# Ranking edges inside a graph network: one copy of the running counts per group, and keys compared with all earlier chunks

## The reference

```python
def spmm(z):
    return jax.ops.segment_sum(edge_weight[:, None] * z[col], row, num_segments=N)
z = x
y = z @ weights[0]
for k in range(1, Kh):          # Kh = 4: three hops
    z = spmm(z)
    y = y + z @ weights[k]
```

## Time and profile before

| what | value |
|---|---|
| median of three runs | 9740.51 us |
| profiled execution, its own time: the span from first to last instruction (nothing around it is recorded) | 12913.0 us |
| stage src_scatter (ranking and scatter by source) | 160 to 1475 us of the span |
| first hop (no ranking) | 1490 to 2720 us |
| second hop, hop1 (100 rankings) | 2734 to 4040 us |
| third hop, hop2 (96 rankings) | 4050 to 5385 us |
| busy share of the span: POOL, PE, DVE, ACT | 54%, 53%, 51%, 16% |

### The profile page before, as it was taken

How to read it: one execution, slowest core, us unless ns; L and a number is a source line. 1 busy time by engine, 2 the same in 40 slices (tenths; PEclk the granted TensorE clock), 3 DMA queues, 4 the chain that set the end, 5 groups by cost and what they waited for, 6 DMA issues and landing times. The chain is left out here.

```text
span 12913.0 us, 169378 instructions
## 1 busy us (share of the span) xinstructions
PE 6851.3 (53%) x37679; PEld 5969.4 (46%) x37680; DVE 6544.7 (51%) x22687; ACT 2092.6 (16%) x6216; POOL 7007.4 (54%) x7417
## 2 busy tenths in 40 slices
PE   6555444445554555356125555566664666655554
PEld 4454333335553555232014445466663556654444
DVE  6444455555555555434125555655555444455555
ACT  4222100001110111011001111222222111122222
POOL 6555566646664666554755555245553455535554
PEclk6555555566666666578557777777777555566676
DMA  0000011111111111223122222111113111122222
GB/s 19 1 1 1 19 45 44 45 42 42 42 42 39 42 42 42 46 70 99 43 48 74 74 74 74 48 35 39 39 39 82 34 37 39 38 53 77 78 79 74
DMA packets 436020, 614.60 MB, mean 48 GB/s; under 512 B 176561, under 2 KB 312069, under 8 KB 435109
## 3 DMA queue, kind: packets, MB, share of 16 engines
q0 software_dynamic: 257024, 486.93, 15.0%
q1 hardware_dynamic: 178305, 119.49, 3.3%
q10 hardware_dynamic: 292, 3.41, 0.1%
HBM read 520.17 MB, written 89.19 MB: 47 GB/s over the span
## 5 line engine op out<-in xcount | busy, mean ns | idle before, releaser
L1098 POOL DMA_INDIRECT hop_rows<-hops,k_src_gather x1568 | 1483.1, 946 | 1037.1 <-issue 438.7
L1149 PE MATMUL hop_sums<-hop_rows,hop_weighted 128*128 x4992 | 1136.9, 399 | 1004.9 <-DVE k_x L1196 678.1
L1149 PEld LDWEIGHTS hop_sums<-hop_rows,hop_weighted 128*128 128x128 f32 x4992 | 990.5, 295 | 1093.3 <-issue 1092.3
L1470 POOL DMA_INDIRECT l_pass_rows<-left_table,k_dst_other x832 | 788.2, 947 | 889.6 <-DVE l_pass_terms L1842 488.2
L1965 POOL DMA_INDIRECT l_weigh_rows<-row_table,l_weigh_ring x832 | 813.3, 978 | 737.8 <-ACT l_weigh_ring L1929 481.4
L1470 POOL DMA_INDIRECT l_pass_rows<-related,k_dst_typed x832 | 787.8, 947 | 740.8 <-DVE l_pass_terms L1842 457.3
L1470 POOL DMA_INDIRECT l_pass_rows<-key_table,k_src_gather x784 | 741.3, 946 | 770.9 <-DVE l_pass_scores L1779 404.8
L728 POOL DMA_INDIRECT src_sorted<-src_scatter_records,src_scatter_places x784 | 752.6, 960 | 583.3 <-DVE src_scatter_places L716 362.5
L1565 PE MATMUL l_pass_sums<-l_pass_zero 128*128 128x272 bf16 (+1 forms) x1210 | 261.2, 305 | 1489.8 <-DVE l_total L1659 1020.4
L1320 POOL DMA_INDIRECT dst_sorted<-rec,dst_places x768 | 760.3, 990 | 525.7 <-issue 225.4
L1098 POOL DMA_INDIRECT hop_rows<-in_x,k_src_gather x784 | 741.4, 946 | 455.0 <-issue 221.0
(11 more groups left out here) (468 smaller groups left out, 18337.5 us busy)
## 6 DMA issues: line engine op xcount, KB each, us to landing
related<-l_tables_rows SPq DMA_DIRECT2D x50, 1024.0 KB
hop_rows<-hops,k_src_gather POOLq DMA_INDIRECT x1568
l_pass_rows<-related,k_dst_typed POOLq DMA_INDIRECT x832
l_pass_rows<-left_table,k_dst_other POOLq DMA_INDIRECT x832
l_weigh_rows<-row_table,l_weigh_ring POOLq DMA_INDIRECT x832
src_sorted<-src_scatter_records,src_scatter_places POOLq DMA_INDIRECT x784
hop_rows<-in_x,k_src_gather POOLq DMA_INDIRECT x784
dst_sorted<-rec,dst_places POOLq DMA_INDIRECT x784
```

The source lines that it names most:

```text
L1098: nc.gpsimd.indirect_dma_start(rows[:, s * G + g, :], None, table_in, bass.IndirectOffsetOnAxis(ap=o.gather[:, c:c + 1], axis=0),).then_in ...
L1149: last = nc.tensor.matmul(sums[:, b, g, :], weighted[:, s % SLOTS, g, :], rows[:, bass.ds(slots[g], 1), :], start=True, stop=True)
L1470: nc.gpsimd.indirect_dma_start(rows[:, s, g, :], None, table, bass.IndirectOffsetOnAxis(ap=index[:, c:c + 1], axis=0),).then_inc(got[s], 16)
```

## The change

In the three rankings (src_scatter, hop1, hop2) the counts are copied once for a group instead of once for a chunk. TensorE adds all four chunks to the counts in a row and raises one signal, and looks all four up in the copy that was made ahead of the group, with one signal. The lookups therefore no longer hold the chunks of the same group, and the comparison makes up for that: chunk g's keys are compared with the key rows of chunks 0 to g, with a mask that is all ones for chunks ahead and the triangle for its own (`k.earlier_ones`). The result tile `same` becomes 16-bit. In a hop, the key rows and the transposes for the next ranking move from TensorE's first half (even step, ahead of chunk 1) to its second half (odd step), behind that step's products.

```diff
@@ scatter_edges and hop: the comparison (VectorE)
-                        nc.vector.scalar_tensor_tensor(out=same[:, g, :], in0=keyrow[:, b, g, :],
-                                                       scalar=records[:, s, g, 0:1], in1=k.before[:],
+                        nc.vector.scalar_tensor_tensor(out=same[:, g * (g + 1) // 2 * P:(g + 1) * (g + 2) // 2 * P],
+                                                       in0=keyrow[:, b, 0:g + 1, :].rearrange("p g j -> p (g j)"),
+                                                       scalar=records[:, s, g, 0:1],
+                                                       in1=k.earlier_ones[:, (G - 1 - g) * P:G * P],
@@ hop: ScalarE, one ranking
-                    for g in range(G):
-                        if g == G - 1:
-                            turn_onehots(r + 1, 1 - b)
-
-                        act.wait_ge(next_ready, r * G + g + 1)
-                        act.wait_ge(looked, r * G + g + 2 * G - 1)
-                        nc.scalar.copy(next_sb[:, g % 2, :], next_ps[:, 0:HIS]).then_inc(next_copied, 1)
+                    act.wait_ge(next_ready, r + 2)
+                    act.wait_ge(looked, r + 2)
+                    nc.scalar.copy(next_sb[:, 1 - b, :], next_ps[:, 0:HIS]).then_inc(next_copied, 1)
+                    turn_onehots(r + 1, 1 - b)
@@ hop: TensorE, rank_columns
                 if half == 0:
+                    pe.wait_ge(next_copied, r + 1)
+                    for g in range(G):
+                        last = nc.tensor.matmul(next_ps[:, 0:HIS], oh_lo[:, s, g, :], oh_hi[:, s, g, :], start=False,
+                                                stop=False, skip_group_check=True)
+                    last.then_inc(next_ready, 1)
+
                     pe.wait_ge(lo_t, r + 1)
                     pe.wait_ge(ranked, r + 1)
-                for g in range(2 * half, 2 * half + 2):
...
+                    for g in range(G):
+                        last = nc.tensor.matmul(nexts[:, b, g, 0:HIS], oh_lo_t[:, b, g, :], next_sb[:, b, :], start=True,
+                                                stop=True)
+                    last.then_inc(looked, 1)
+                else:
+
+                    pe.wait_ge(taken, r + 1)
+                    pe.wait_ge(onehots, r + 2)
+                    pe.wait_ge(matched, r + 2)
+                    for g in range(G):
+                        last = nc.tensor.transpose(keyrow[:, g, :], column[:, b, g:g + 1].to_broadcast([P, P]), k.ident[:])
+                    last.then_inc(rows_ok, 1)
```

More of the change, by code:

```diff
@@ L172, in _ @@
                                     base=0, pattern=[[-1, P]], channel_multiplier=1)
-            nc.gpsimd.affine_select(out=k.before[:], in_=k.before[:], compare_op=ALU.is_gt, fill=0.0,
+            nc.gpsimd.affine_select(out=k.before, in_=k.before, compare_op=ALU.is_gt, fill=0.0,
                                     base=0, pattern=[[-1, P]], channel_multiplier=1).then_inc(made, 1)
@@ L515, in _ @@
     def _(pe):
-        nc.tensor.transpose(turned[:], k.before[:], k.ident[:]).then_inc(pe_step, 1)
+        nc.tensor.transpose(turned[:], k.before, k.ident[:]).then_inc(pe_step, 1)
         pe.wait_ge(d, 2)
@@ L589, in scatter_edges @@
         picked = sb("picked", [P, G, HIS])
-        same = sb("same", [P, G, P])
+        same = sb("same", [P, sum(range(G + 1)) * P], BF16)
         base = sb("base", [P, 2, G])
@@ L659, in _ @@
                     for g in range(G):
[L661 to L674, removed]
+                        last = nc.tensor.matmul(nexts[:, b, g, 0:HIS], oh_lo_t[:, b, g, :], next_sb[:, b, :], start=True,
+                                                stop=True)
+                    last.then_inc(looked, 1)
+                    pe.wait_ge(taken, n + 1)
+                    pe.wait_ge(onehots, n + 2)
+                    for g in range(G):
+                        last = nc.tensor.transpose(keyrow[:, b, g, :], records[:, s, g, 0:1].to_broadcast([P, P]), k.ident[:])
+                    last.then_inc(rows, 1)
+                    turn_onehots((s + 1) % SLOTS)
         @block.vector
@@ new lines, in rank_columns @@
+                    for g in range(G):
+                        last = nc.tensor.matmul(nexts[:, b, g, 0:HIS], oh_lo_t[:, b, g, :], next_sb[:, b, :], start=True,
+                                                stop=True)
+                    last.then_inc(looked, 1)
+                else:
+                    pe.wait_ge(taken, r + 1)
+                    pe.wait_ge(onehots, r + 2)
+                    pe.wait_ge(matched, r + 2)
+                    for g in range(G):
+                        last = nc.tensor.transpose(keyrow[:, g, :], column[:, b, g:g + 1].to_broadcast([P, P]), k.ident[:])
+                    last.then_inc(rows_ok, 1)
+                    for g in range(G):
+                        last = nc.tensor.transpose(turned[:, 1 - b, g, :], oh_lo[:, (s + 1) % SLOTS, g, :], k.identb[:])
+                    last.then_inc(turned_ok, 1)
@@ L1211, in rank_same @@
                 for g in range(G):
-                    last = nc.vector.scalar_tensor_tensor(out=same[:, g, :], in0=keyrow[:, g, :],
-                                                          scalar=column[:, b, g:g + 1], in1=k.before[:],
+                    last = nc.vector.scalar_tensor_tensor(out=same[:, g * (g + 1) // 2 * P:(g + 1) * (g + 2) // 2 * P],
+                                                          in0=keyrow[:, 0:g + 1, :].rearrange("p g j -> p (g j)"),
+                                                          scalar=column[:, b, g:g + 1],
+                                                          in1=k.earlier_ones[:, (G - 1 - g) * P:G * P],
                                                           op0=ALU.is_equal, op1=ALU.mult,
```

59 lines of the change are left out of this document (25 added, 34 removed).

## The result

| | median | lowest to highest | runs |
|---|---|---|---|
| before | 9742.35 us | 9735.38 to 9761.99 | 4 |
| after | 9971.19 us | 9960.04 to 9973.62 | 4 |

The change makes the kernel 2.3% slower: the ratio, estimated from all the runs, is 1.0228, with a 95% interval of 1.0216 to 1.0241; the two medians lie 229 us apart. The profiled execution of after has a span of 9958.3 us, so its idle times are, other than those of the recording before (12913.0 us), those of the runs.

What follows compares the result with a forecast made beforehand. POOL's indirect DMAs were taken to bound the kernel, 9.42 us a pair of steps. A 10.5 us loop gave 196 x (10.5 - 9.42) = 212 us on 9740.5, about 9950 us; range 9735 to 10110, the forecast's own 9800 to 10090.

Steps and rivals of the forecast that it cites:

- POOL bounds before, and the recording's waits are not in the runs: All three ranking stages: POOL issues indirect DMAs nearly without a break, 9.42 us for a pair of steps in a hop.
- Longer comparisons, 0.67 us taken: VectorE in each ranking: 768 more columns at 0.87 ns each, so comparisons go from 1.09 to 1.76 us.
- One copy and one signal worth nothing: ScalarE makes one copy instead of four, TensorE three hand-overs less; at POOL's pace worth nothing in the runs.
- src_scatter unchanged: src_scatter: VectorE's 3.7 us and TensorE's 3.8 us plus at most 0.6 a group stay below POOL's 5.04; nothing changes.
- faster: Rival, chance 0.11: real chunk-by-chunk waits go, 90 us vanish in src_scatter if a quarter is real; 9650 us.
- The two engines take turns: Hops: VectorE 3.90 us, then TensorE 6.84 us, a loop of 10.74 us over POOL's 9.42; 10.5 after adjustments.
- TensorE's clock, minus 0.55 us: Hop loop: products n + 2 and key rows run at the higher clock level half of the time, minus 0.55 us.
- nothing moves: Rival: clock rises, loop 8.79 us, POOL stays the bound, 9740 us; chance 0.19 including a loop at 9.4 to 9.5.
- Register loads, plus 0.3 us: Hop loop: a third of TensorE's 0.94 us a pair of register loads ahead of products counts, plus 0.3 us.
- POOL's waits do not soften it: Hops: products hold back POOL's ring, so POOL falls back too and the 212 us arrive in full.
- slower still: Rival: POOL's own pace below 1.25 us, say 1.17; the loop costs 333 us, 10075 us; chance 0.70 together with the forecast.
- The change doesn't do what it says: Rival, chance given only as "hardly": TensorE's list shows key rows behind the products and the four lookups together.

## Why the prediction was right

It said 9950 us and slower; it is 9971, for the reason given. That the number came so near is luck: the cost of the rankings was put about 105 us too low, and some 90 us that come back at the ends of the hops were left out.

- **POOL bounds before, and the recording's waits are not in the runs: right.** I had derived 9.42 us for a pair of steps from single durations; the recording without the long waits gives 9.48 by its gathers.
- **Longer comparisons, 0.67 us taken: too little.** The starts of the four are 0.27, 0.41, 0.54 and 0.67 us apart in after, 1.89 us together against 1.09 in the earlier trace rows: 0.80 us. The slope of the earlier trace rows, worked out between an operation with a running sum and one without, was the wrong neighbour. The Trainium skill's figure (VectorE: DVE Perf Modes, The TRN2 errata), by which I had estimated 0.80, agrees.
- **One copy and one signal worth nothing: right as it was put,** at POOL's pace (ratio 1.0009 with the key rows early). It isn't nothing in a loop of two engines, where it saves 0.24 us by hiding register loads.
- **src_scatter unchanged: right.** From its first scatter to its last it takes 988.7 us after and 990.7 before; POOL's waits for places fell from 67.8 to 21.8 us, but most of them were hardly longer than the pause that follows an issue in any case, and this speaks against the rival *faster*. That line's instructions in after (min/median/max ns, first and last start), with its waits for places (us, times):

```profile
L731 POOL DMA_INDIRECT src_sorted<-src_scatter_records,src_scatter_places x784: 954/958/1201, 159.1 to 1147.8; - x196
...
  DVE src_scatter_places L719: 21.8, 4
```

  The same of the kernel before, recorded once more:

```profile
L728 POOL DMA_INDIRECT src_sorted<-src_scatter_records,src_scatter_places x784: 957/962/1204, 160.4 to 1151.1; - x196
...
  DVE src_scatter_places L716: 67.8, 158
```

- **The two engines take turns: right,** piece by piece as listed, and shown by taking the key rows back (no cost) and by lengthening one piece (the time grows by it).
- **TensorE's clock, minus 0.55 us: wrong.** The second half of the burst stayed at the lower level. The stretches of after's turn (us, TensorE busy (count), granted clock, DMA share, GB/s):

```profile
2709.80:2713.10 3.30, 0.19 (x4) 1.00 0.23 60
2713.20:2716.80 3.60, 2.82 (x16) 0.50 0.26 55
2716.80:2720.60 3.80, 3.80 (x20) 0.50 0.13 35
2720.69:2724.00 3.31, 0.39 (x4) 0.50 0.24 59
```

  In 2713.20 to 2720.60 the granted clock is 0.50, the 1.2 GHz level, and the products take 1.86 and 1.83 us. In this turn the 2.4 GHz level came at the end of a burst, by 2709.80, as TensorE went into its 3.99 us of waiting, and was gone when the work began; behind the next burst, at 2720.69, it did not come at all. So the rival *nothing moves* fell. The Trainium skill (TensorE: Matmul & The Clock Gate, Part 1) says that sustained activity releases the clock; the trace agrees with it for the one burst, where the release came too late to serve, and not for the next. In 2250 to 3050 us nearly all turns had their second half at the lower level: the key rows there took 420 ns a matmul, 1.06 us for four, where at the higher level four take 0.61 us (before, recorded again, at 3206.38 us).

```profile
L1137 PE MATMUL hop_keyrow<-k_ident,hop_column 128*128 128x128 f32 x296 | 78.3, 420 | 0.0
```

- **Register loads, plus 0.3 us: wrong for after,** where they run while the lookups do; in the two kernels with four copies they stand open for 0.84 and 0.87 us.
- These terms together put the loop at 10.5. With 0.13 us for the comparisons, without the clock's 0.55 and the register loads' 0.3 it would have been 10.87; it is 10.93. The rest is small: VectorE's two pieces with the hand-over to the products took 2.34 us where the sum had 2.14, and the lookups took 1.92 us where it had 2.08.
- **"POOL's waits do not soften it": wrong.** Two things soften it, at the ends of both hops. This table cuts each hop into pieces, of before (recorded again) and after:

| us | hop1 before | hop1 after | hop2 before | hop2 after |
|---|---|---|---|---|
| first gather to first comparison | 28.9 | 32.1 | 19.3 | 22.5 |
| first to last comparison | 918.0 | 1082.9 | 887.3 | 1039.3 |
| last comparison to last products | 35.5 | 18.6 | 75.5 | 36.6 |
| last products to hop2's first gather, or to the destination scatter | 30.4 | 18.0 | -1.6 | -24.8 |
| sum | 1012.9 | 1151.6 | 980.6 | 1073.6 |

  The rankings cost 317 us more. Behind the last of them hop1 has 8 more steps and hop2 has 16: in after these find their rows gathered and take 2.1 us each, in before they wait for POOL, about 5 us each, and this gives 56 us back. After's timeline at the two ends:

```profile
3297.58 1.15 PE L1154 MATMUL hop_sums<-hop_rows,hop_weighted 128*128 x8 [0.33 <-DVE k_x L1201]
...
4388.02 0.94 POOL L1101 DMA_INDIRECT hop_rows<-hops,k_src_gather  x1 [0.30 <-issue]
4389.26 0.99 POOL L1327 DMA_INDIRECT dst_sorted<-rec,dst_places  x1 [0.30 <-issue]
...
4411.92 1.15 PE L1154 MATMUL hop_sums<-hop_rows,hop_weighted 128*128 x8 [0.97 <-DVE k_x L1201]
4414.04 1.15 PE L1154 MATMUL hop_sums<-hop_rows,hop_weighted 128*128 x8 [0.97 <-DVE k_x L1201]
```

  The same of the kernel before, recorded once more:

```profile
3151.63 2.07 PE L1149 MATMUL hop_sums<-hop_rows,hop_weighted 128*128 x8 [2.94 <-SPq L1285]
...
4159.30 2.07 PE L1149 MATMUL hop_sums<-hop_rows,hop_weighted 128*128 x8 [2.92 <-SPq L1285]
4164.20 2.07 PE L1149 MATMUL hop_sums<-hop_rows,hop_weighted 128*128 x8 [2.83 <-SPq L1285]
```

  The second thing is POOL's own work behind its last gather, which does not wait for TensorE's last steps. At the end of hop2 POOL goes on to the scatter by destination while TensorE has 26 us of steps left; in before it is 3 us. At the end of hop1 POOL scatters 16 chunks before hop2 starts: in after this ends beside TensorE's last products (3280.77 to 3299.74), in before it lies behind them (3150.14 to 3171.90). Together this gives 36 us back.

Together with 6 us in the first row that is 317 + 6 - 56 - 36, or 232 us before rounding, from the first gather of hop1 to the scatter by destination; 229 us were measured for the whole. The forecast's 212 us lacked the 105 us by which the rankings cost more (0.43 us a turn for the longer loop, and the rankings of before took 9.26 and 9.33 us, not 9.42) and the 91 us that come back.

The rival *slower still* wanted a POOL pace below 1.25 us, and it is 1.257. *The change doesn't do what it says* is out as well.

What stays open: whether the loop would be hidden with TensorE at its higher level, since no kernel with late key rows had that, and what the transposes' place alone does, since no run moves them without the key rows.

## What to carry to other kernels

Ask of every instruction that is moved which engine waits for its result, and what that engine has queued behind the wait: here key rows that were made a step ahead of their use became the last piece of a burst for which VectorE waits, and two engines with 7.3 and 7.5 us of work, side by side under a bound of 9.5 us, became one loop of 10.9. Work that is added beside another engine's bound costs nothing (0.80 us a ranking: ratio 1.0002), and the same work in such a loop costs all of itself. Take a loop's length from the first and the last of its instructions over a whole stage; single turns were off by up to 0.16 us. And look at the ends of a stage: what a loop adds there can lie beside work that does not wait for it (36 us here).

## What the runs showed that I had not expected

- The same kernel was recorded with a span of 12913.0 us and of 9732.6 us. A gather took 946 ns in both; the idle time before the 1568 gathers was 1037.1 and 486.9 us. So one recording added idle time and left the durations as they are.
- Two more counts and lookups between the products cost less than nothing: with two of them 2.15 us passed there, with four 1.92, since the 0.84 to 0.87 us of TensorE's own issue ahead of the second products then lay beside them.
- In the turn shown, TensorE's granted clock went to its higher level just as the engine fell idle, and was back at the lower one when its work began.
